# Moving the low halves of four blocks of rows from GpSimd to VectorE in the first stage of a fused attention and mixture-of-experts kernel

## The reference, cut to what matters

```
xn = layernorm(x)
off = xn @ W_off + b_off ; w = softmax(xn @ W_attn + b_attn)      # attention: positions and weights
logits = xn @ router_w.T + expert_bias ; top 2 of 8 experts       # routing
out = x + attention(off, w, xn[:, 0, :]) @ W_out + b_out + shared_ffn(xn) + routed_ffn(xn, top 2)
```

## Time and profile before

| | us |
|---|---|
| median of 3 runs | 399.27 (399.08 to 399.86) |
| the profiled execution | 399.35 |
| its span, first to last instruction | 397.5 |
| TensorE busy in the span | 360.5 |
| VectorE busy | 310.6 |
| GpSimd busy | 236.7 |
| ScalarE busy | 185.4 |

### The profile page before, as it was taken

How to read it: one execution, slowest core, us unless ns; L and a number is a source line. 1 busy time by engine, 2 the same in 40 slices (tenths; PEclk the granted TensorE clock), 3 DMA queues, 4 the chain that set the end, 5 groups by cost and what they waited for, 6 DMA issues and landing times.

```text
span 397.5 us, 12279 instructions
## 1 busy us (share of the span) xinstructions
PE 360.5 (91%) x4303; PEld 312.3 (79%) x4303; DVE 310.6 (78%) x846; ACT 185.4 (47%) x434; POOL 236.7 (60%) x200
## 2 busy tenths in 40 slices
PE   0166998998999999999999999999999999999993
PEld 0064675665767777777789999999999999999992
DVE  5988888978989999999967788666666666666663
ACT  2667842767344677777665444222222232222220
POOL 1555902157787773343106999188866767667676
PEclk9996999999999999999999999999999999999998
DMA  8954520001154797758663656666565555653333
GB/s 294 297 133 108 127 89 2 0 23 57 50 121 120 172 193 152 166 136 160 134 124 84 194 183 126 138 84 71 65 73 56 62 60 61 61 60 30 30 34 32
DMA packets 99157, 41.34 MB, mean 104 GB/s; under 512 B 73888, under 2 KB 92704, under 8 KB 99104
## 3 DMA queue, kind: packets, MB, share of 16 engines
q1 hardware_dynamic: 87408, 31.82, 35.0%
q0 software_dynamic: 11264, 8.69, 16.5%
q10 hardware_dynamic: 432, 0.11, 0.2%
HBM read 10.94 MB, written 12.88 MB: 60 GB/s over the span
## 4 chain that ended last, share of the span: by engine, by line
PE 81%; DVE 10%; POOL 3%; DMA 2%; issue 2%; ACT 1%; DVEq 0%; POOLq 0%; ACTq 0%
PE pY L863 18%; PE pY L696 12%; PE pAB L839 9%; PE pAB L837 9%; PE pAB L838 9%; PE pAB L684 6%; PE pAB L686 6%; PE pAB L685 6%; PE pV L708 4%; DVE hot L1201 2%; DVE hbuf L1291 1%; DMA base<-in_x 1%; POOL units L1109 1%; DMA xT<-hot 1%; POOL rows L1101 1%
## 5 line engine op out<-in xcount | busy, mean ns | idle before, releaser
L1154 POOL DMA_INDIRECT out_dram<-xT,rows x64 | 98.9, 1545 | 46.5 <-DVE xT L1653 26.6
L1145 POOL DMA_INDIRECT sorted_rows<-rows,slot x64 | 70.5, 1102 | 51.6 <-DVE hbuf L1291 38.5
L1088 ACT ACTIVATE units<-pAB 128x512 f32<-128x512 f32 x78 | 46.4, 594 | 108.9 <-PE pAB L839 93.1
L837 PE MATMUL pAB<-rows,wsp 128*128 128x128 f16 x512 | 87.6, 219 | 0.0
L838 PE MATMUL pAB<-rows,wsp 128*128 128x128 f16 x512 | 87.6, 219 | 0.0
L839 PE MATMUL pAB<-rows,wsp 128*128 128x128 f16 x512 | 87.6, 219 | 0.0
L1591 DVE SCALAR_TENSOR_TENSOR hbuf<-pAB,units 128x512 f32<-128x512 f32 x78 | 53.6, 687 | 37.6 <-PE pAB L839 37.2
L863 PE MATMUL pY<-wsp,hbuf 128*128 (+1 forms) x620 | 78.7, 279 | 0.5 <-issue 0.4
L863 PEld LDWEIGHTS pY<-wsp,hbuf 128*128 128x128 f32 x620 | 72.7, 192 | 0.8 <-issue 0.8
L696 PEld LDWEIGHTS pY<-wsp,hbuf 128*128 128x128 f32 x512 | 66.7, 191 | 8.3
L696 PE MATMUL pY<-wsp,hbuf 128*128 128x128 f32 x512 | 68.0, 276 | 0.0
(11 more groups left out here) (166 smaller groups left out, 588.4 us busy)
## 6 DMA issues: line engine op xcount, KB each, us to landing
base<-in_x SPq DMA_DIRECT2D x8, 512.0 KB, 7.4
out_dram<-base SPq DMA_DIRECT2D x16, 256.0 KB, 2.5
wraw<-in_wall SPq DMA_DIRECT2D x10, 256.0 KB, 3.1
rows<-hot SPq DMA_DIRECT2D x8, 256.0 KB, 2.7
proj<-sorted_rows SPq DMA_DIRECT2D x27, 68.5 KB, 1.9
wsp<-in_wall SPq DMA_DIRECT2D x10, 128.0 KB
sorted_rows<-rows,slot POOLq DMA_INDIRECT x64, 2.5
out_dram<-xT,rows POOLq DMA_INDIRECT x64, 3.4
```

The source lines that it names most:

```text
L837: pe.matmul(o, hi, x(0), start=True, stop=False)
L1088: nc.scalar.activation(silu[:, q % 2, 0:job.cols], pAB[:, 2 * (q % 2), 0:job.cols], ACT.Silu, scale=1 / (XS * WS)).then_inc(d_silu, 1)
L1145: pool.indirect_dma_start(sorted_rows, bass.IndirectOffsetOnAxis(ap=slot[:, t:t + 1].bitcast(U32), axis=0), rows[:, t, :], None, bounds_ch ...
L1154: pool.indirect_dma_start(out_rows, bass.IndirectOffsetOnAxis(ap=meta[:, t, DEST - CW:DEST - CW + 1].bitcast(U32), axis=0), yt[:, t], None ...
```

## The change

VectorE makes the low halves of blocks 9, 11, 13 and 15, each right behind its own cast of the block and ahead of everything else of that step in its queue; GpSimd leaves these four out. A second semaphore, `own_lo`, counts them, and everything that waited for a low half waits for the one of the two that counts that block (`low_made`): SyncE's transposes, TensorE's `turn`, and the two normalisations that reuse the place in the ring.

```
+OWN_LOWS = (9, 11, 13, 15)
+        def low_made(eng, i):
+            if i in OWN_LOWS:
+                eng.wait_ge(own_lo, OWN_LOWS.index(i) + 1)
+            else:
+                eng.wait_ge(rows_lo, i + 1 - sum(b < i for b in OWN_LOWS))
...
             for k in range(SENT):
-                sp.wait_ge(rows_lo, 2 * k + 1)
+                low_made(sp, 2 * k)
...
                 k = i // 2
-                pe.wait_ge(rows_lo, i + 1)
+                low_made(pe, i)
...
                 if i >= 4:
-                    act.wait_ge(rows_lo, i - 3)
+                    low_made(act, i - 4)
...
             def rows_low(g, r):
                 i = 4 * g + r
+                if i in OWN_LOWS:
+                    return
                 pool.wait_ge(rows_hi, i + 1)
...
                 if i >= 4:
-                    pool.wait_ge(rows_lo, i - 3)
+                    low_made(pool, i - 4)
...
                 v.tensor_copy(halves(i)[:, :, 0, :], xs[:, r, :, :]).then_inc(rows_hi, 1)
+                if i in OWN_LOWS:
+                    low, high = (halves(i)[:, :, s, :] for s in (1, 0))
+                    dve.wait_ge(rows_hi, i + 1)
+                    v.tensor_tensor(low, xs[:, r, :, :], high, ALU.subtract).then_inc(own_lo, 1)
```

More of the change, by code:

```diff
@@ L388, in layer_kernel @@
         rows_lo = sem("rows_lo")
+        own_lo = sem("own_lo")
         turned = sem("turned")
```

## The result

The changed kernel took 402.8 us (402.2 to 403.29, four runs) against 399.27 (399.08 to 399.86): a ratio of 1.0082, with an interval of 1.0067 to 1.0097. The forecast was 400.7. The direction was right and the size was not: 3.5 us were added where 1.4 were foreseen, and the time lies above the range.

The account below looks back on a forecast made before the run. The prediction took three nearly level engines to bound the first stage, which sets the routing's start; VectorE's added work and GpSimd's holds summed to +1.4 us, 400.7 against a median of 399.27, range 398.8 to 401.9.

Parts of the forecast that it names:

- Block 9 is free: First stage, VectorE: block 9's own low half costs nothing, since 1.40 us of idle time follow.
- 0.73 us a block on VectorE: First stage: each own low half, 0.69 us plus 0.04 wait, moves everything behind it on VectorE by 0.73 us.
- the sum: First stage's delays added along VectorE's queue to the routing: +1.34 or +1.48 us, taken as +1.4.
- The cast of block 13 held by subtraction 12: First stage: VectorE's cast waits for GpSimd's subtraction, to 45.03, and ends at 45.32 instead of 44.59 us.
- the first: Rival at block 13's cast: not held, so GpSimd's relief is a gain; 399.0, or as likely 399.4 us; chance 0.12.
- the second rival: First stage: GpSimd holds only VectorE's two-input instructions, not casts; +0.5, 399.8 us; chance 0.19.
- The cast of block 15 held by subtraction 14: First stage: VectorE's cast is held by GpSimd to 49.11 and ends at 49.40 instead of 48.04 us.
- The routing 1.34 later: End of first stage: VectorE's routing arithmetic starts at 54.54 against 53.20 us.
- the third rival: TensorE's granted clock falls between 42 and 56 us, adding 2 to 3 us: 402.7 to 403.7; chance 0.07.
- Later stages are shifted whole: After the routing's start: all later work moves by the first stage's delay, with no cost of its own.

Follow-up runs that it names:

- the added products: Changed kernel with 22 identity products on TensorE ahead of block 11's turn: 402.52 us; with sixteen unread counter increments on GpSimd as well: 401.36 us.
- 12 to 16 increments left out: Kernel before with 12, 14 or 16 of GpSimd's counter increments taken out of the first stage: 398.88, 398.93 and 399.38 us.
- the added increments: Changed kernel with sixteen increments of a counter that nobody reads in GpSimd's queue behind the first stage: 401.18 us, ratio 1.0049.
- block 9; 13 and 15: Changed kernel with only block 9's low half on VectorE: 399.83 us; with only those of blocks 13 and 15: 400.04 us.
- ten increments out: Kernel before with ten of GpSimd's sixteen counter increments taken out of the first stage: 401.0 us, ratio 1.0017.

## Why the prediction was wrong, step by step

- **Block 9 is free.** Right: 0.03 us of stage.
- **0.73 us a block on VectorE.** The cast of block 12 came 0.60 later, measured from the last scale (7.01 and 6.41). A little too much: the copy behind the subtraction starts 0.08 before its end (41.58 + 0.69, then 42.19), and the sum had put the next instruction 0.04 after it.
- **The cast of block 13 held by subtraction 12, ending 0.29 after it.** Right: 0.28; 0.29 with the added products. This settles the first and the second rival: the cast was not let through, and nothing was gained at block 13. The Trainium skill, page "SBUF — State Buffer", section "Who interferes with whom", lets a cast in VectorE's two-port mode stand still for the whole of a GpSimd instruction; the 1.13 to 1.24 us of held casts agree. For the own low half of block 13 the sum had 46.1 as its end; it was 46.01 (46.37 less 0.36). The cast of block 14 came at 47.24 (47.60 less 0.36), where 47.3 was foreseen.
- **The cast of block 15 held by subtraction 14, to 49.40.** In the profiled execution this step failed: it waited for ScalarE, behind a silu that waited for products at half speed, and ended at 49.99 (50.35 less 0.36). Where the clock stayed up, it was held for 1.17 and ended at 49.27 on the same scale.
- **The routing 1.34 later.** Without the fall of the clock 1.10 (three runs, 18.18 to 18.19 against 17.09); with it 1.83. The term was sized well, and what came on top was the sign of the third rival, to which I gave 0.07 on the argument that as much work lay in the stretch as before. That the measured 402.8 lies in the rival's range of 402.7 to 403.7 is luck: it asked for 2 to 3 us of added low clock, and the clock cost 0.73, at 0.79 over 32 to 48 us as before. Why the low clock came later is open; gaps of the same size stood in an execution without it.
- **"Later stages are shifted whole."** This is the step that failed most, and the one that put the time above the range: the sum gave what comes after the stage nothing of its own. The rest of the span is 1.61 longer. The forecast counted the change's instructions by their time and not by their place in GpSimd's code: fewer of them ahead of the sort move a load of instructions from 48 us to between the sort's release and its first row. The Trainium skill, page "Runtime: NRT & Kernel Launch", section "Instruction fetch mechanics", has the cost of crossing a block of instructions as mostly hidden. Here the rows agree before, and with 12 to 16 increments left out, where the second row came in time; with the load between release and first row it cost the second row 0.53 to 0.82 us, and the rest of those executions is 0.9 to 1.8 longer. Of the rest's 1.61 after the change not all is the late issue: the 31st row was issued 1.06 late, and it landed some 1.5 later after its issue than before.

In the measured times the added 3.5 us part so: the added increments take 1.6 off (402.8 to 401.2; the intervals of the two ratios, 1.0067 to 1.0097 and 1.0032 to 1.0066, just don't meet), which the profiles put into the sort and the wait behind it. The 1.7 that stay above the kernel before on the same chip (401.18 against 399.51) are by the profile 1.1 of VectorE's queue, forecast as 1.4; the clock and waits for the 31st row may make the remainder, which was not tried apart. That run's interval, 1.3 to 2.6 us, holds the forecast.

What stays open: how often the clock falls where it costs time, since one profiled execution of the changed kernel shows it, one with the added increments alone does not, and the medians with and without the added products (402.52 and 402.8; 401.36 and 401.18) don't separate. The spans, without the time outside them, have medians of 400.4 and 401.05, 398.9 and 399.4: shorter with the products by some 0.5, from too few executions to call it shown. And why the 31st row lands late. In three profiled executions with that row on time (block 9; 13 and 15; ten increments out) it is issued at 73.73 to 73.88, as in the kernel before, lands 4.12 to 4.44 after its issue, and VectorE waits 1.6 to 2.0; their rests are 345.0 to 345.3. In the four with the row late (74.9) it lands 3.7 to 4.0 after its issue, VectorE waits 2.5 to 2.8, and the rests are 345.9 to 346.1. Without such a wait the rests are 344.2 to 344.3, but for the one with the fallen clock. What the landing competes with was not tried apart.

None of these versions is shown to beat the kernel before; twelve or fourteen increments fewer come nearest, with intervals that reach 1.0004 and 1.0001.

## What to carry to other kernels

Idle time on an engine pays for added work only if what comes next can start when that work is done: VectorE had 0.62 us to spare at block 13, but its cast then met a GpSimd instruction that moves with the same work, and the spare time went into the hold. A late stage is not a shift of all that follows: look for what races against another queue downstream (here the 31st sorted row against VectorE's overwriting). And when instructions are added to or taken from an engine, look where its instruction loads fall in the new trace before blaming the order; a few increments without effect, added or left out, tell the two apart.

## What the runs showed of the hardware that was not expected

- A load of GpSimd's instructions that lies between a release and the indirect DMA behind it goes with a first row that starts 2.0 to 2.2 us after the load's start, 1.59 to 1.66 after its end; the load itself lasts 0.34 to 0.56. The first row is 1.9 to 2.2 later than before by it, and only 0.5 to 0.8 us of that reach the second row, since VectorE would have held the first one for 1.4.
- One increment left out moved that load by some 0.3 us from twelve on (30.1, 30.7 and 31.2 with 12, 14 and 16 out), and by 0.1 between eight and ten (29.2 to 29.4).
- The hold between VectorE and GpSimd works on the sort too. The first row took 2.63 under VectorE's subtraction of 2.28 and 1.23 behind it; with the subtraction moved, the third row took 2.42. A delay of 0.65 us became 1.46 at the eighth row, where VectorE's two-input instructions caught another row, and 1.06 at the 31st, and a start 1.40 us early was lost again at the third.
- GpSimd's tile normalisations hold VectorE less than its subtraction does. The own low half of block 13 was issued in a pair of them (45.23, 1.48) and took 0.82 instead of 0.69.
